# Mamba block with a mixture of experts on eight cores: the experts' first product by pairs of chunks, stored by token, gathered by block

## What is computed

```python
xn = layernorm(x)                                   # [16, 2048, 1024]
out = x + ssm(xn) + ffn(xn)

# ssm: 8 groups of 128 channels, 16 states each
u, v = split(xn @ in_proj_w.T + in_proj_b)
delta = softplus(u @ delta_proj_w.T)
B = u @ b_proj_w.T + b_proj_b                       # per group of channels, 16 states
uc = silu(causal_conv4(u) + conv_b)
h = exp(delta * A) * h + (delta * uc) * B           # over time, for each of 1024 x 16 states
y = sum_n(h * c_param) * silu(v)

# ffn: a shared expert, and 2 of 8 experts for each token
shared = swiglu(xn @ w_shared_in) @ w_shared_out
w = top2(softmax(xn @ w_gate + gate_bias))
hid = swiglu(xn @ w1_shared)                        # one first product for all experts
routed = sum_e(w[:, e] * (hid @ w2[e]))
```

## Time and profile before

| what | value |
|---|---|
| median of 3 runs | 2320.32 us (2319.33 to 2324.01) |
| the profiled execution | 2307.04 us |
| its span on the slowest core (core 2) | 2304.3 us |
| spans of the eight cores | 2276.8 to 2304.3 us |
| first scan starts | 137.55 us |
| busiest engines | DVE 75%, PE 74%, POOL 65%, ACT 57% |
| DMA | 579.09 MB, mean 251 GB/s |

### The profile page before, as it was taken

How to read it: one execution, slowest core, us unless ns; L and a number is a source line. 1 busy time by engine, 2 the same in 40 slices (tenths; PEclk the granted TensorE clock), 3 DMA queues, 4 the chain that set the end, 5 groups by cost and what they waited for, 6 DMA issues and landing times.

```text
span 2304.3 us, 34679 instructions; the slowest of 8 cores (2276.8 to 2304.3 us)
## 1 busy us (share of the span) xinstructions
PE 1708.9 (74%) x8595; PEld 729.0 (32%) x8595; DVE 1726.8 (75%) x2078; ACT 1315.7 (57%) x2075; POOL 1491.3 (65%) x1363
## 2 busy tenths in 40 slices
PE   5456556564698988987798897888898969764664
...
GB/s 204 228 177 257 192 193 153 214 272 287 202 207 283 226 272 259 256 219 284 231 275 294 285 327 245 269 265 331 254 287 307 310 288 255 232 233 274 286 240 178
DMA packets 134953, 579.09 MB, mean 251 GB/s; under 512 B 24546, under 2 KB 25954, under 8 KB 92002
## 3 DMA queue, kind: packets, MB, share of 16 engines
...
## 4 chain that ended last, share of the span: by engine, by line
PE 33%; DMA 33%; issue 10%; DVE 9%; ACT 5%; SPq 5%; POOL 4%; DVEq 1%; ACTq 0%; POOLq 0%
PE pw L639 8%; DMA ddscr<-dd 6%; PE pw L665 5%; PE pw L626 5%; DMA part<-acc 5%; DVE hsc L1144 5%; PE pw L579 4%; DMA xn_r<-xscr 4%; DMA out<-xt 4%; PE pw L595 3%; DMA bb<-bscr 2%; DMA out<-area 2%; POOL dBu L1219 2%; PE pw L603 2%; DMA wsb<-ring 2%
## 5 line engine op out<-in xcount | busy, mean ns | idle before, releaser
L1219 POOL TENSOR_TENSOR dBu<-rep,bb 128x512 bf16<-128x512 bf16 x1024 | 1168.4, 1154 | 572.0 <-DVE hsc L1144 538.5
L1144 DVE TENSOR_TENSOR_SCAN hsc<-pdA,st,dBu 128x512 bf16<-128x512 f32 x768 | 956.3, 1271 | 237.1 <-ACT pdA L832 172.9
L832 ACT ACTIVATE pdA<-rep,A_sb 128x512 f32<-128x512 bf16 x1024 | 693.4, 686 | 495.4 <-DVE hsc L1144 471.5
L1144 DVE TENSOR_TENSOR_SCAN hsc<-pdA,dBu 128x512 bf16<-128x512 f32 x256 | 303.8, 1211 | 72.5 <-ACT pdA L832 59.6
L639 PE MATMUL pw<-ring,area 128*128 128x512 bf16 x1120 | 273.3, 388 | 44.8 <-ACT area L733 36.6
L626 PE MATMUL pw<-ring,area 128*128 128x512 bf16 x864 | 221.1, 403 | 60.4 <-DVE acc L949 34.3
L665 PE MATMUL pw<-xn_r,ring 128*128 128x512 bf16 x832 | 224.5, 419 | 25.6 <-DVE mid L943 9.3
L746 ACT ACTIVATE th<-pw 128x512 f32<-128x512 f32 x256 | 150.3, 590 | 97.1 <-PE pw L597 36.5
L579 PE MATMUL pw<-xn_r,ring 128*128 128x512 bf16 x480 | 127.7, 418 | 99.9 <-DMA xn_r<-xscr 83.1
L639 PEld LDWEIGHTS pw<-ring,area 128*128 128x128 bf16 x1120 | 106.2, 99 | 181.1 <-issue 70.2
L651 PE MATMUL pw<-xn_r,ring 128*128 128x512 bf16 x480 | 131.0, 422 | 22.4 <-DVE sv L921 9.7
...
## 6 DMA issues: line engine op xcount, KB each, us to landing
ring<-wsb SPq DMA_DIRECT2D x110, 1024.0 KB
rep<-ddscr SPq DMA_DIRECT2D x256, 256.0 KB
bb<-bscr SPq DMA_DIRECT2D x256, 128.0 KB
xt<-wsb SPq DMA_DIRECT2D x20, 1024.0 KB
...
wsb<-ring SPq DMA_DIRECT2D x17, 1024.0 KB, 14.0
acc<-x SPq DMA_DIRECT2D x8, 2048.0 KB, 14.0
```

The costliest lines, as they stand in the source:

```text
L832: sc.activation(pdA[:, j % 2, :], rep[:, G % 2, n % 4, 0, :], AF.Exp, scale=A_sb[:, G % 8, n:n + 1]).then_inc(s_da, 1)
L1144: v.tensor_tensor_scan(hsc[:, n, :], pdA[:, j % 2, :], dBu[:, j % NDB, :], init, ALU.mult, ALU.add).then_inc(s_scan, 1)
L1219: gp_.tensor_tensor(dBu[:, j % NDB, :], rep[:, G % 2, n % 4, 1, :], bb[:, G % 2, n // 4, :], ALU.mult).then_inc(s_dbu, 1)
```

## The change

- **First product.** `xn_f` holds two chunks at a time. A pair of chunks is normalised and transposed straight into it, 92 slots for a pair, and `HA`/`HB` of the pair follow at once in 86 slots (27 to 113, 119 to 205, 211 to 297, 303 to 389). The reload of `xscr` remains for chunk 0 alone.
- **Stored by token.** Each `HB` writes a tile of 128 x 512 into one of two buffers, and SyncE stores it to `htok` in token order (64 plain DMAs, `hst`). The scatters and the zero-fill are gone.
- **Token numbers in lists.** `RK` moves from slot 112 to 333. After it GpSimd scatters the number of each token into a list by row, `rtok` (64 indirect DMAs of 128 numbers, one in each slot from 337 on), which SyncE loads into `rtk`.
- **Rows gathered by block.** GpSimd fetches the rows of a block from `htok` through `rtk` (78 indirect DMAs, `rows_in`), in place of SyncE's 78 plain ones. Expert blocks start in slot 426 and end in 884.
- **Prologue.** The second piece of `DL` goes to `mid`, so its cast waits for nothing. The load of `cmat`, the casts that need a stored piece and most stores move behind the eight delta groups. `acc<-x` moves from slot -20 to 4.
- The sixth ring slot opens in slot 337 in place of 116.

```diff
@@ build_plan @@
-            put(T_X + L_X * (c - 1) + 0.25 * L_X * i, ("XT", c, i, 0, None, 3))
+            put(ln_slot(c) + 6 * i, ("XT", c, i, 0, None, 3))
...
-    spread(hid, T_H0, T_HID)
+    for p in range(NCH // 2):
+        hid = [(k, c, i, h, P_H + 2 * h + (k == "HB"), 8) for h in range(2)
+               for c in (2 * p, 2 * p + 1) for i in range(4) for k in ("HA", "HB")]
+        spread(hid, T_X + L_P * p + 24, T_X + L_P * p + 110)
...
-T_X, L_X, T_H0, T_HID, T_EX = 3, 15, 118, 430, 880
+T_X, L_P, T_EX0, T_EX = 3, 92, 426, 884
+def ln_slot(c):
+    return T_X + L_P * (c // 2) + (24 if c % 2 and c > 1 else 0)
...
-POOL_EV += [(gslot(("HB", c, i, 1)) + 3, ("scat", c, i)) for c in range(NCH) for i in range(4)]
-POOL_EV += [(gslot(("RK", 0, 0, 0)) + 3 + k, ("zf", k)) for k in range(NZ)]
+POOL_EV += [(gslot(("RK", 0, 0, 0)) + 4 + n, ("id", n)) for n in range(2 * NT)]
+POOL_EV += [(max(T_EX0 - 9, gslot(("RT", q // 2 - 2, q % 2, 0)) + 2 if q >= 4 else 0),
+             ("rows", q)) for q in range(2 * NBK)]
...
-POOL_EV += [(-59, ("consts",))]
+POOL_EV += [(-59, ("wbp",)), (-3, ("cmat",))]
...
+    if _id == P_DL + 1 and _id not in FIRST:
+        _open = [RING + 1]
...
-            POOL_EV.append((_t + 3 if _t > -40 else _t, ("cast", _p)))
-        _SP.append((_use + 1 if _by == "sw" else -39, ("store", _p)))
+            POOL_EV.append((max(_t + 3, -3) if _t > -40 else _t, ("cast", _p)))
+        _SP.append((_use + 1 if _use > -4 else -12 if _id in (P_U, P_U + 1) else 2,
+                    ("store", _p)))
...
-    _SP.append((128 * _c + 11 if _c else -20, ("xacc", _c)))
+    _SP.append((128 * _c + 11 if _c else 4, ("xacc", _c)))
...
+_SP += [(gslot(("HB",) + key) + 3, ("hst", n)) for key, n in HQ.items()]
@@ VectorE, HB @@
-                        if c and b == 0:
-                            need(v, "DVE", s_sc[a], 32 * c)
-                        ins = v.scalar_tensor_tensor(hid[:, a, 512 * b:512 * (b + 1)],
+                        n = HQ[(c, a, b)]
+                        if n >= 2:
+                            need(v, "DVE", s_hst[n % 2], 16 * (n // 2))
+                        ins = v.scalar_tensor_tensor(hid[:, n % 2, :],
@@ GpSimd @@
-                    for k in range(2):
-                        gp_.indirect_dma_start(hrow_h, at(idx[:, k, T:T + 1]), hid[:, i, :], None
-                                               ).then_inc(s_sc[i], 16)
+                    gp_.indirect_dma_start(rtok_h, at(idx[:, k, T:T + 1]), tk[:, T:T + 1], None
+                                           ).then_inc(s_id_row, 16)
+                def rows_in(q):
+                    j, t = divmod(q, 2)
+                    need(gp_, "POOL", s_rtk, 16)
+                    for r in range(2):
+                        need(gp_, "POOL", s_hst[r], 16 * (len(HQ) // 2))
+                    if q >= 4:
+                        need(gp_, "POOL", s_grp, GI[("RT", j - 2, t, 0)] + 1)
+                    gp_.indirect_dma_start(rows[:, q % 4, :], None, htok_h, at(rtk[:, j, t:t + 1])
+                                           ).then_inc(s_rows[q % 4], 16)
@@ SyncE @@
+                    elif kind == "hst":
+                        c, i, h = HORD[n]
+                        need(s, "SP", s_vev, V_IDX[GI[("HB", c, i, h)]] + 1)
+                        r0 = 128 * (4 * c + i)
+                        s.dma_start(htok_h[r0:r0 + 128, 512 * h:512 * (h + 1)], hid[:, n % 2, :]
+                                    ).then_inc(s_hst[n % 2], 16)
```

More of the change, by code:

```diff
@@ L157, with tok_tile @@
 X6 = (gslot(("RK", 0, 0, 0)) + 4, CSLOT[0] - 20)
+HQ = {}
+for _k, _c, _a, _b, _p, _t in GROUPS:
+    if _k == "HB":
+        HQ[(_c, _a, _b)] = len(HQ)
+HORD = sorted(HQ, key=HQ.get)
+XB = [q if q < 4 else (q - 4) % 3 for q in range(NT)]
+XPREV = [max([p for p in range(q) if XB[p] == XB[q]], default=None) for q in range(NT)]
+XN = [sum(XB[p] == XB[q] for p in range(q + 1)) for q in range(NT)]
+def tok_tile(c, i):
+    return 1 if c == 0 and i % 2 else 0
+TOK_PREV = {}
+_lastt = {}
+for _c in range(NCH):
+    for _i in range(4):
+        TOK_PREV[(_c, _i)] = _lastt.get(tok_tile(_c, _i))
+        _lastt[tok_tile(_c, _i)] = (_c, _i)
 def norm_slot(c, i):
@@ L177 @@
     + [(norm_slot(c, i), ("lnn", c, i)) for c in range(NCH) for i in range(4)]
-    + [(gslot(("XT", c, 3, 0)) + 2, ("xst", c)) for c in range(NCH)]
+    + [(gslot(("XT", c, 3, 0)) + 2 if c else 0, ("xst", c)) for c in range(NCH)]
     + [(-30, ("A",))]
@@ L185 @@
 DVE_EV = table(
-    [(norm_slot(c, i) - 7, ("lns", c, i)) for c in range(NCH) for i in range(4)]
+    [(norm_slot(c, i - i % 2) - 5 + i % 2, ("lns", c, i)) for c in range(NCH) for i in range(4)]
     + [(rstd_slot(c, h) - 1, ("vpe", c, h)) for c in range(NCH) for h in range(2)]
@@ L208 @@
 SLOT_OF, FORMER, USED_AT = [], [], []
[L209 removed]
+_last = [None] * (RING + 2)
 for _p, _id in enumerate(PIECES):
@@ L262 @@
     _SP.append((max(16 * (_G - 1), gslot(("BP", _c, 0, 0)) + 3), ("bb", _G)))
-for _q in range(NX, NT):
-    _SP.append((norm_slot(*divmod(_q - NX, 4)) + 1, ("xt", _q)))
+for _q in range(4, NT):
+    _SP.append((max(norm_slot(*divmod(XPREV[_q], 4)) + 1, -6), ("xt", _q)))
 SP_EV = table(_SP)
@@ L269 @@
 C_PK = C_JJ + NBK
-N_CST = C_PK + 16
+C_TK = C_PK + 16
+N_CST = C_TK + NT
 def _pk(w):
@@ L488, in build @@
         s_wex = [sem("s_wex%d" % p) for p in range(2 * E)]
-        s_sc = [sem("s_sc%d" % r) for r in range(4)]
-        s_zf = sem("s_zf")
+        s_hst = [sem("s_hst%d" % r) for r in range(2)]
+        s_id_row, s_rz, s_rtk = sem("s_id_row"), sem("s_rz"), sem("s_rtk")
+        s_rzm = sem("s_rzm")
         s_rows = [sem("s_rows%d" % r) for r in range(4)]
@@ L1251, in _ @@
             def _(s):
-                for q in range(NX):
+                for q in range(4):
                     s.dma_start(xin[q], x_rows(q // 4, q % 4, 1).squeeze(1)).then_inc(s_xt[q], 16)
```

189 lines of the change are left out of this document (78 added, 111 removed).

## The result

The changed kernel takes 2487.5 us (median of 4 runs, 2477.4 to 2514.2) against 2322.2 us for the kernel before on the same chip: a ratio of 1.073, 95% interval 1.063 to 1.084. It is 7% slower; 2288 us, faster, with a range of 2238 to 2340 us was forecast. The profiled execution took 2487.37 us, the span of its slowest core is 2484.7 us. Medians here are over all executions of a kernel, while ratios leave out those of a slower state, in which the cores of one die or of both need some per cent more, often at a lower clock; of the profiled executions that with 8 bytes between the words and that with added transfers are touched by it.

What follows compares the result with a forecast made beforehand. Up to 1120 us VectorE with waits was taken as the bound, TensorE behind it. 135 + 714 + 152 + 56 + 21 = 1078 us against 1120, less 10 us behind: 32 us off 2320.32, so 2288 us, range 2238 to 2340.

Steps and rivals of the forecast that it cites:

- part 3 of the sum: Slots 337 to 401: one indirect DMA per drive, GpSimd the bound at 2.37 us each, 152 us.
- First scan 135: Prologue: two waits go, but casts waiting for stores delay the first drive; first scan at 135 us, gain 2.5 us.
- Slots 0 to 337: Before the list's slots: VectorE busy 640 us, idle 0.22 us per slot or 74 us, sum 714 us; lateness of 21 separate.
- no wait for a reload: Sign for slots 0 to 337: 2.1 us each, VectorE about 90% busy, with no wait for a reload.
- the late `SO` piece: Second `SO` piece, cast in slot 109 and used in 111: 4.3 us for a landing of 12.9, 9 us late.
- the stores to `htok`: At slots 139 and 267 SP's wait behind `part<-acc` holds these stores; 3 us taken for each.
- Nothing: Rival, 8%: VectorE's work up to slot 434 unchanged, idle 0.30 us per slot, every late piece felt; 2320 us.
- Expert blocks: After the list: 78 more indirect DMAs, 92 us of GpSimd, cost 10 us; 1.96 to 2.0 us per slot.
- VectorE's wait for drives: Sign in the expert blocks: waits near 25 us; the prediction is wrong if over 60.
- Slower by GpSimd: Rival, 13%: row gathers wait for TensorE's transposes in the expert blocks; 2343 us with 65 us exposed, 2370 with all.
- slower by the two buffers: Rival, 10%: stores from the two `hid` buffers land in 18 us, each of 32 pairs waits 2 us; 2352 us.
- the four: The prediction's rivals: one faster than forecast (17%, 2228 us), one without gain (8%), two slower (13% and 10%).

Runs made afterwards that it cites:

- folded kernel: Changed kernel with its 40 KB list of 4-byte elements dealt out so consecutive rows lie 312 bytes apart; 2358.2 us, ratio to before 1.0185.

## Why the prediction was wrong

- **The step that failed is part 3 of the sum, the list.** It priced the 64 indirect DMAs on the engine that describes them, by the earlier trace rows, where each writes 2048-byte rows, and took "GpSimd's time is that of describing 128 rows". That was right: 157 us measured once the words are apart, 152 forecast. But it gave the writes themselves no price, to other transfers or at the memory. The rows of before show scattered writes of 2 KB only; 4-byte ones side by side were outside them, and the range held no bound for their effect on others. They cost all other transfers of the slowest core three times their time, and 64 slots 286 us instead of 157. That is 129 of the 213 us, shown by folding the same 40 KB (2487 to 2358 us).
- *A page's rule.* The Trainium skill (DMA: Bandwidth & Descriptors, Specifications) asks for transfers of 512 bytes or more for full rate, and says that smaller ones are done by reading, changing and writing back. That is a rule on a transfer's own rate; what a small write costs others does not go by size in the runs: 4 bytes and 512 bytes cost them the same (52 and 50 engine-us per MB). If smaller writes are read-modify-writes, then runs of them side by side would have to queue for each other, which would fit the column of the table; that is only argued.
- **First scan 135, measured 156.7.** The mechanism was seen and its wait too short. More to the point, the term itself was no term: a scan 15 us earlier was worth nothing at slot 64. The sum should have priced what waits for transfers up to slot 64, not the gate alone.
- **Slots 0 to 337.** VectorE's busy time came out at 642.3 us (305.18 + 337.13) against 640 forecast. The idle time was mis-sized: 138 us instead of 74 + 21, that is 0.41 us per slot. The forecast took its 0.26 from 660 to 1120 us of before, past the stretch with 0.47. Some of it by name (total, times, longest), and the first wait as it was before:

```profile
PE pw L613 <- DMA xn_r<-xscr: 38.6, 3, 23.9
...
PE pw L708 <- DMA ring<-wstream: 13.0, 1, 13.0
...
DVE area L973 <- DMA htok<-area: 7.1, 2, 4.7
```

```profile
PE pw L579 <- DMA xn_r<-xscr: 42.4, 3, 21.0
```

  The reload of `xscr` held TensorE 23.9 us in one piece, much as before (21.0), where "no wait for a reload" was forecast; the late `SO` piece cost TensorE 13.0 where 9 were forecast; the stores to `htok` cost 7.1, near the 6 forecast. If these three are all felt, the rest is near 0.3 us per slot, which is what the rival "Nothing" assumed.
- **Expert blocks, right.** 2.00 us per slot, and VectorE's wait for drives 25.1 us, forecast near 25. From slot 434 on the folded kernel needs 1191 us, forecast 1184 + 10.
- **Rivals.** "Slower by GpSimd" and "slower by the two buffers" did not happen: the gathers of rows cost what was forecast, and in the folded kernel a store to `htok` lands in 3.1 us at the median in the list's slots and in 7.7 us in slots 64 to 336, under the 16 us that it has. The Trainium skill's sum of 2.0 us and the bytes at 436 GB/s (DMA: Bandwidth & Descriptors, Anatomy of one DMA), from which the prediction estimates 2.3 us, is a fit to DMAs issued by GpSimd, and this store is SyncE's; the 7.7 us measured decides. The outcome had a mechanism that none of the four had.
- **Without the touching words** the change is still not a gain: 2358.2 against 2312.6 us, 1.0185. By the starts of scans in the two profiled executions, 41 us of span: 7 at slot 336 (937.4 against 930.3), 37 in the 64 slots of the list (158 against 121), 13 less in the next 32, 10 more behind. The list's 64 instructions stand in 64 slots, so GpSimd's turn shows in full.
